# Four units of 448 targets summed from fetched rows as the stationary operand, and routing and experts in one block

## The chip, the cores and the metric

The kernel runs on one core of a Trainium2 chip. The metric is the device time of one execution in microseconds. The engines are TensorE (PE, whose weight loads the profile lists apart as PEld), VectorE (DVE), ScalarE (ACT), GpSimd (POOL) and SyncE (SP), which here only issues DMAs. Each runs its own instructions in order and waits on semaphores.

## What is computed

A layer of a graph transformer on 6,250 nodes with 256 features. Two graph convolutions (`arma_conv`, three steps and two stacks each), an attention block without softmax, and a mixture of six experts of which each node takes two. The part that the change rewrites is the sum over edges in the first convolution:

```python
def arma_conv(x, edge_src, edge_dst, init_w, w, root_w, b, num_layers=T):
    dinv = jnp.where(deg > 0, deg ** (-0.5), 0.0)
    norm = dinv[edge_src] * dinv[edge_dst]
    root = jnp.einsum('nf,kfg->nkg', x, root_w)
    for t in range(num_layers):
        h = (jnp.einsum('nf,kfg->nkg', x, init_w) if t == 0
             else jnp.einsum('nkf,kfg->nkg', out, w))
        msg = h[edge_src] * norm[:, None, None]
        h = jax.ops.segment_sum(msg, edge_dst, num_segments=n)
        out = jax.nn.relu(h + root + b[None])
    return out.mean(axis=1)
...
xn = _layernorm(x)
x = x + gnn(xn, edges) + mix(xn)
x = x + moe(_layernorm(x))      # softmax router, top 2 of 6 experts, three layers each
```

There are 106,250 edges (50,000 random ones in both directions and a loop at each node), sorted by target.

## The kernel before

Nodes lie in 49 tiles of 128 (`TILES`), or in 14 windows of 448 (`WIN`), two of which make a pair of 7 tiles. A table of features holds, for each node, 2 x 128 features in fp16 as a high and a low part, 512 values in all. The stages follow one another:

- *Preparation* (to about 334 us): the layer norm, the root products, the attention sums, and on the side the lists of edges.
- *Build* (334 to 1030 us): PE builds the dense 6272 x 6272 adjacency matrix in fp16 from one-hots (196-column matmuls, L1821 and L1825, a fresh 128x128 load before each), stores it window by window as `adj_d`, and sums the convolution's first step from it (L1836).
- *Pass 0 and pass 1* (`quick_pass`, 1035.8 to 1552.3 and to 2078.5 us): the second and third step of the first convolution. Here the targets are parted. Targets of the dense windows (5 to 13, 9 in all, `DENSE`) are summed by `tile_sums`: for each of 49 source tiles, four matmuls (two stacks, two parts) with the features as 128x128 stationary operand and 448 columns of `adj_d` moving (L1886). The first 2,304 targets, 18 tiles (`SPARSE`), are summed without the matrix: GpSimd fetches the rows of 128 edges' sources by an indirect DMA into one of 16 buffers `got` (L1345), DVE makes a 128x128 one-hot of the edges' targets (L1632), and PE multiplies: one-hot stationary, the 512 fetched values moving (L1932). Two tiles (a duo) share 36 such chunks, 324 a pass; four chunks of a duo serve both tiles, so there are 360 matmuls. Window 5 overlaps these targets by 64 columns, so its matmuls have 384 columns.
- *Late passes* (2078.5 to about 2858 us): the second convolution, all 14 windows dense, in hardware loops, with PE running freely.
- *Decode and routing* (`final`), then *experts* in a block of their own: each token's row is scattered twice into its experts' regions (`row_d`) and 38 slots of 384 rows are computed.

The code of passes 0 and 1 is unrolled. `Course` sets its order: for each step x (a window's tile; 9 x 49 = 441 steps a pass) it says which chunk, transpose and row product follow the tile's four matmuls. Chunks start after step 28. After a tile's last chunk, ACT and DVE scale its sums (`sums_high`, `sums_low`), PE transposes them (`sums_turned`, L1940), DVE adds the root (`sums_hidden`), and PE makes the next features (`row_products`, L1899, in pass 1 L1901 and L1904) in one of two PSUM banks, which ACT and DVE read out (L1427, L1639). A dense window ends with six DVE operations (`finish`).

SP refills `stage0` in pieces of 7 tiles (784 KB, L1314), counted through both passes, 63 a pass. For piece M it waits until PE has used M - 6 pieces (`p_free`). Between them it loads roots and stores pass 0's new features (`some_out`, L1299) to `later_d`. GpSimd begins pass 1 only when all those stores have landed (`t_rows`). A flag makes the kernel take `slow_pass` where a tile has more edges than its chunks hold.

## Time and profile before

| what | us |
|---|---|
| median of 3 runs (3478.55 to 3478.9) | 3478.65 |
| the profiled execution | 3479.78 |
| its span, first to last instruction | 3477.8 |
| build, 333.7 to 1029.7 | 696.0, PE busy 675.85 |
| pass 0, 1035.8 to 1552.3 | 516.5, PE busy 459.98 |
| pass 1, 1552.3 to 2078.5 | 526.2, PE busy 478.63 |
| late passes, 2078.5 to 2858.0 | 779.5, PE busy 773.39 |
| decode and routing, 2858.0 to 3140.8 | 282.8, PE busy 178.09 |
| experts, 3140.8 to the end | 337.0, PE busy 322.51 |

PE is busy for 91% of the span. Its matmuls overlap, so one that is listed with 0.35 us may follow its neighbour after 0.19 us: the starts tell the pace, not the durations. "Idle before" is the time for which an engine had nothing to run ahead of an instruction, with what ended it; "issue" means that nothing that the profile shows was waited for.

### The profile page before, as it was taken

Reading aid. Unit: us, or ns where it says so; the run is one execution under the profiler, and the core shown is the slowest. Engines: PE = TensorE matmul, PEld = TensorE weight load, DVE = VectorE, ACT = ScalarE, POOL = GpSimd, SP = SyncE. Lnnn points to the kernel's source line nnn. Section 1 sums busy time; section 2 is a strip of 40 time slices with the busy share of each in tenths; the row PEclk is TensorE's granted clock in tenths of the full one; section 3 lists DMA queues with packets and bytes.
Section 4 is the critical chain, followed back from the end, with each engine's and each line's share of the span. In section 5 each row is a group of like instructions: output and inputs, shape, how many; then the busy total and the mean of one; then the engine's idle time right before and its main releaser. Section 6 shows DMA issues by size and latency. Waiting matters only on the chain. (4 is left out here: it accounts for less than half of the span.)

```text
span 3477.8 us, 48392 instructions
## 1 busy us (share of the span) xinstructions
PE 3163.9 (91%) x16879; PEld 1851.0 (53%) x16880; DVE 1374.4 (40%) x5337; ACT 787.6 (23%) x1656; POOL 923.7 (27%) x912
## 2 busy tenths in 40 slices
PE   7798999999998898898999999999999999728998
PEld 3464666566554444454455555555555556516775
DVE  7846777777732222221222221222221005433443
ACT  3444555555520000000000000000000003313332
POOL 2000000000006666636666630000000000454555
PEclk9897999999998999999999999999999999869999
DMA  7212465556457666756666668888889995336886
GB/s 185 72 65 85 149 235 208 179 198 234 179 234 246 196 222 203 235 179 203 211 211 223 212 188 291 291 290 292 291 292 319 303 302 160 118 111 168 204 203 138
DMA packets 252700, 723.78 MB, mean 208 GB/s; under 512 B 36437, under 2 KB 159817, under 8 KB 250472
## 3 DMA queue, kind: packets, MB, share of 16 engines
q1 hardware_dynamic: 184298, 595.84, 51.1%
q0 software_dynamic: 53216, 112.76, 11.7%
q10 hardware_dynamic: 15006, 12.82, 1.3%
q8 instruction: 109, 1.79, 0.2%
q14 instruction: 71, 0.58, 0.0%
HBM read 543.01 MB, written 189.34 MB: 211 GB/s over the span
## 5 line engine op out<-in xcount | busy, mean ns | idle before, releaser
L1886 PE MATMUL first_sum<-stage,split 128*128 128x448 f16 (+1 forms) x4508 | 933.3, 355 | 31.4 <-issue 29.1
L1886 PEld LDWEIGHTS first_sum<-stage,split 128*128 128x128 f16 x4508 | 443.6, 99 | 448.4 <-issue 63.7
L1886 PE MATMUL first_sum<-stage,other 128*128 128x448 f16 (+1 forms) x3136 | 664.8, 354 | 15.7 <-issue 15.5
L1836 PE MATMUL first_sum<-stage,other 128*128 128x448 f16 x2744 | 649.9, 354 | 0.2 <-ACT stage L1360 0.2
L1345 POOL DMA_INDIRECT stage<-fresh_d,lane_two x324 | 308.4, 952 | 1117.2 <-DMA fresh_d<-split 942.0
L1886 PEld LDWEIGHTS first_sum<-stage,other 128*128 128x128 f16 x3136 | 309.6, 99 | 298.3 <-issue 35.4
L1360 ACT ACTIVATE stage<-group_ps 128x392 f16<-128x392 f32 x784 | 385.4, 497 | 297.9 <-PE group_ps L1825 294.7
L1345 POOL DMA_INDIRECT stage<-later_d,lane_two x324 | 307.7, 950 | 220.4 <-issue 71.5
L1513 DVE TENSOR_SCALAR place<-iota_col,rel 128x196 f16<-128x196 f16 x1568 | 348.8, 265 | 0.0
L1836 PEld LDWEIGHTS first_sum<-stage,other 128*128 128x128 f16 x2744 | 254.0, 98 | 139.5 <-issue 2.0
L1932 PE MATMUL group_ps<-stage,place 128*128 128x512 f16 x720 | 265.8, 385 | 11.3 <-issue 7.3
L1510 DVE TENSOR_TENSOR lanes<-iota_two,lane_two 128x256 f16<-128x256 f16 x784 | 225.0, 287 | 83.3 <-PE group_ps L1825 71.5
L1821 PE MATMUL group_ps<-place,lanes 128*128 128x196 f16 x784 | 199.9, 255 | 33.4 <-DVE place L1513 14.7
L2247 POOL IOTA ids<- 128x49 f32 x1 | 0.2, 173 | 841.2 <-POOLq L1233 841.2
L2751 POOL DMA_INDIRECT out<-slot_out,slot_idx x114 | 176.5, 1548 | 163.9 <-DMA out<-slot_out,slot_idx 92.7
L1632 DVE TENSOR_SCALAR place<-iota_col,lane_two 128x128 f16<-128x128 f16 x720 | 145.8, 272 | 156.8 <-PE group_ps L1932 111.9
L1825 PE MATMUL group_ps<-place,lanes 128*128 128x196 f16 x784 | 200.9, 257 | 0.0
L2360 ACT ACTIVATE dT<-d_ps,rel 128x448 f32<-128x448 f32 x14 | 8.8, 633 | 843.2 <-PE d_ps L2278 814.1
L1710 DVE TENSOR_TENSOR stage<-first_sum,stage 128x448 f32<-128x448 f32 x42 | 26.2, 625 | 390.7 <-PE first_sum L1886 377.0
L1821 PEld LDWEIGHTS group_ps<-place,lanes 128*128 128x128 f16 x784 | 77.7, 99 | 113.5 <-ACT stage L1360 43.5
L2716 DVE TENSOR_TENSOR slot_out<-out_ps,other 128x256 f32<-128x256 f32 x114 | 48.4, 425 | 185.7 <-PE out_ps L2826 180.0
L2263 POOL DMA_INDIRECT row_d<-rows,seat_idx x84 | 83.8, 998 | 126.0 <-DVE seat_idx L2526 101.9
(387 smaller groups left out, 3052.6 us busy)
## 6 DMA issues: line engine op xcount, KB each, us to landing
stage<-adj_d SPq DMA_DIRECT2D x420, 784.0 KB
adj_d<-stage SPq DMA_DIRECT2D x14, 5488.0 KB, 18.5
row_d<-slow_rows SPq DMA_DIRECT2D x12, 3340.5 KB
other<-pack_d SPq DMA_DIRECT2D x38, 898.0 KB
slot_rows<-row_d SPq DMA_DIRECT2D x38, 393.0 KB
stage<-root_d SPq DMA_DIRECT2D x18, 448.0 KB
xnT_d<-other SPq DMA_DIRECT2D x14, 448.0 KB
split<-root_d SPq DMA_DIRECT2D x14, 448.0 KB, 3.8
```

What stands on the lines that cost most here:

```text
L1345: nc.gpsimd.indirect_dma_start(got[:, g % GOT, :, :].rearrange("p s c -> p (s c)"), None, tables_d[t].rearrange("p j s c -> (p j) (s c)"), ...
L1360: nc.scalar.activation(stage[w % 2][:, :, at * G:(at + 1) * G], group_ps[g % BANKS][:, 0:COLS].rearrange("p (d h) -> p h d", d=G), ACT.Cop ...
L1510: nc.vector.tensor_tensor(lanes[:, u % 4, :, :], iota_two[:, :, :], lane_two[:, bass.ds(g, 1), :].broadcast_to([P, P, 2]), ALU.is_equal)
L1513: nc.vector.tensor_scalar(place[:, 2 * u % RING + s, :], iota_col[:, 0:Q4], rel[:, :, :, :].rearrange("p q s g -> p (q s g)")[:, bass.ds(p ...
L1632: nc.vector.tensor_scalar(hot[:, h % HOTS, :], iota_col[:, s % 2 * P:s % 2 * P + P], tab_key[:, at:at + 1], None, ALU.is_equal).then_inc(s ...
L1821: mm(group_ps[u % BANKS][:, 0:Q4], lanes[:, u % 4, :, 0], place[:, 2 * u % RING, :], start=True, stop=True, skip_group_check=True)
L1825: return mm(group_ps[u % BANKS][:, Q4:COLS], lanes[:, u % 4, :, 1], place[:, 2 * u % RING + 1, :], start=True, stop=True, skip_group_check ...
L1836: m = mm(acc[b][k][:, 0:WIN], other[:, h, half, k * P:(k + 1) * P], stage[b][:, h, :], start=(h == 0 and half == 0), stop=(h == TILES - 1 ...
L1886: m = mm(acc[b][k][:, lo:WIN], side(t)[:, h, part, k * P:(k + 1) * P], ring[:, i, r, lo:WIN], start=(h == 0 and part == 0), stop=(h == TIL ...
L1932: m = mm(group_ps[S % 2][:, :], hot[:, h % HOTS, :], got[:, g % GOT, :, :].rearrange("p s c -> p (s c)"), start=(n == SPANS[s % 2][0]), st ...
L2263: nc.gpsimd.indirect_dma_start(row_d[:, :], bass.IndirectOffsetOnAxis(ap=seat_of[:, j, which:which + 1], axis=0), rows[:, j, :], None).the ...
L2751: nc.gpsimd.indirect_dma_start(out[:, :], bass.IndirectOffsetOnAxis(ap=idx[:, b, t:t + 1], axis=0), done[:, b, t, :], None, bounds_check=N ...
```

## The change

*Targets.* The parted targets are now 4 whole windows ("units") of 448, 1,792 in all. The dense windows are 4 to 13, ten, all 448 wide, so a pass has 490 steps and 70 pieces. A unit is 4 strips of 112 targets with 17 chunks each: 16 x 17 = 272 fetches a pass.

*Chunk.* The fetched rows are the stationary operand (four 128x128 blocks: two stacks, two parts) and the one-hot of 112 targets moves: four matmuls of 112 columns. The sums come out with features on the partitions, so the transposes and the scaling on ACT go; DVE finishes a strip in three operations (`strip_finish`). There are 8 buffers for fetched rows instead of 16, and GpSimd also waits for the former fetch into the same buffer.

*Order.* `Course` has TAIL 22 for 14 and LEAD 10 for 7. The table's parts are stored by pair (`pair_out`), after the load of the piece with the same number; a piece number is now `x // PT + PIECES + 1`, where it was `x // PT + PIECES - 1`.

*Routing and experts.* The experts' instructions follow the routing's on each engine in the same block, and all 98 scatters are in one sequence on GpSimd. SP waits for a semaphore that DVE raises when the table of slots is ready. Buffers of the experts lie in `split`'s space, PSUM banks are shared.

```diff
-SPARSE = 18
-FIRST_DENSE = SPARSE * P // WIN
-CHUNK = 36
-SPANS = (range(0, 19), range(15, CHUNK))
+UNITS = 4
+STRIP = 112
+STRIPS = WIN // STRIP
+CHUNK = 17
+LISTED = UNITS * STRIPS * CHUNK
...
-        return x // PT + PIECES - 1
+        return x // PT + PIECES + 1
...
-                def some_out(n):
-                    if n < PARTED:
-                        sp.wait_ge(s_rows, n + 1)
+                def pair_out(pair):
+                    if pair < UNITS // 2:
+                        sp.wait_ge(s_rows, pair + 1)
                     else:
-                        sp.wait_ge(d_rows, n - PARTED + 1)
-                    js = slice(SOME[n][0], SOME[n][-1] + 1)
+                        sp.wait_ge(d_rows, pair - UNITS // 2 + 1)
+                    js = slice(pair * SUB, (pair + 1) * SUB)
                     sp.dma_start(tables_d[1][:, js, :, :], other[:, js, :, :]).then_inc(t_rows, 16)
...
-                        for some in range(len(SOME)):
-                            if M == stored_at(some):
-                                some_out(some)
                         if M >= PIECES:
                             sp.wait_ge(p_free, M - (PIECES - 1))
                             sp.dma_start(ring[:, i, :, :].rearrange("p t n -> p (t n)"), adj_d[DENSE[n], :, i * PT * WIN:(i + 1) * PT * WIN]).then_inc(p_in[i], 16)
...
+                        for pair in range(PAIRS):
+                            if M == stored_at(pair):
+                                pair_out(pair)
...
-                        if g >= GOT:
-                            pool.wait_ge(s_used, g - (GOT - 1))
-                        at = listed_at(c)
+                        if g >= RING:
+                            pool.wait_ge(s_used, g - (RING - 1))
+                            pool.wait_ge(s_row[g % RING], 16 * (g // RING))
...
+                def strip_finish(t, s):
+                    S, at = t * PARTED + s, s % STRIPS * STRIP
+                    one = hid_s[:, :, s % (2 * STRIPS) * STRIP:(s % (2 * STRIPS) + 1) * STRIP]
+                    ps = group_ps[S % 2][:, :].rearrange("p (k c) -> p k c", k=2)[:, :, 0:STRIP]
+                    if s % STRIPS == 0:
+                        dve.wait_ge(s_in, 32 * (t * UNITS + s // STRIPS + 1))
+                    dve.wait_ge(s_used, t * LISTED + (s + 1) * CHUNK)
+                    nc.vector.tensor_tensor(one, ps, dinv_s[:, at:at + STRIP].unsqueeze(1).broadcast_to([P, 2, STRIP]), ALU.mult).then_inc(s_ev, 1)
+                    dve.wait_ge(s_ev, S + 1)
+                    nc.vector.tensor_tensor(one, one, rin_s[:, :, at:at + STRIP], ALU.add).then_inc(s_v, 1)
+                    dve.wait_ge(s_v, S + 1)
                     nc.vector.tensor_scalar(one, one, 0.0, None, ALU.max).then_inc(s_hid, 1)
...
                 def chunk(t, c):
                     g = t * LISTED + c
-                    pe.wait_ge(s_row[g % GOT], 16 * (g // GOT + 1))
-                    for s in tiles_of(c):
-                        S, n, p = t * SPARSE + s, c % CHUNK, PRODUCTS.index((c, s))
-                        h = t * len(PRODUCTS) + p
-                        if n == SPANS[s % 2][0] and S >= 2:
-                            pe.wait_ge(s_v, S - 1)
-                        pe.wait_ge(s_hot, h + 1)
-                        m = mm(group_ps[S % 2][:, :], hot[:, h % HOTS, :], got[:, g % GOT, :, :].rearrange("p s c -> p (s c)"),
-                               start=(n == SPANS[s % 2][0]), stop=(n == SPANS[s % 2][-1]), skip_group_check=True)
+                    s, first = divmod(c, CHUNK)
+                    S = t * PARTED + s
+                    if first == 0 and S >= 2:
+                        pe.wait_ge(s_ev, S - 1)
+                    pe.wait_ge(s_hot, g + 1)
+                    pe.wait_ge(s_row[g % RING], 16 * (g // RING + 1))
+                    for k in range(2):
+                        for part in range(2):
+                            m = mm(group_ps[S % 2][:, k * D:k * D + STRIP], got[:, g % RING, part, k * P:(k + 1) * P], hot[:, g % HOTS, :],
+                                   start=(first == 0 and k == 0 and part == 0), stop=(first == CHUNK - 1 and part == 1), skip_group_check=True)
                     m.then_inc(s_used, 1)
...
-                    for n in range(BATCHES - 1):
+                    for n in range(BATCHES):
                         scattered(n)
+                    slots.gpsimd(pool)
...
+                    dve.sem_inc(l_table, 1)
+                    slots.vector(dve)
```

PE at the start of pass 0's chunks, before; L1932 is a chunk, L1886 the dense sums of one tile (x4):

```order
L1932 MATMUL group_ps<-stage,place 128x512
L1886 MATMUL first_sum<-stage,split 128x384 x4
L1932 MATMUL group_ps<-stage,place 128x512
L1886 MATMUL first_sum<-stage,split 128x384 x4
L1932 MATMUL group_ps<-stage,place 128x512
```

The same place after; L1874 is a chunk, L1832 the dense sums:

```order
L1874 MATMUL group_ps<-place,stage 128x112 x4
L1832 MATMUL first_sum<-stage,split 128x448 x4
L1874 MATMUL group_ps<-place,stage 128x112 x4
L1832 MATMUL first_sum<-stage,split 128x448 x8
L1874 MATMUL group_ps<-place,stage 128x112 x4
```

One matmul became four, the first window's tiles are wider, and chunks lie further apart (1.62 steps for 1.23).

SP around the end of pass 0, before; `later_d` is the table of pass 1, and its last store is the second of these:

```order
L1299 DMA later_d<-other 128x2048
L1314 DMA stage<-adj_d 128x3136 x3
L1299 DMA later_d<-other 128x3584
L1314 DMA stage<-adj_d 128x3136
L1280 DMA stage<-root_d 128x2x448
```

The same after; the last row here is the last store:

```order
L1267 DMA later_d<-other 128x3584
L1275 DMA stage<-adj_d 128x3136 x3
L1247 DMA stage<-root_d 128x2x448
L1248 DMA stage<-dinv_d 128x448
L1275 DMA stage<-adj_d 128x3136 x2
L1267 DMA later_d<-other 128x3584
```

The last store stood ahead of piece 71, the ninth of a pass of 63, and now stands behind piece 80, the eleventh of a pass of 70.

GpSimd from the last routing to the experts, before; `row_d` takes the tokens' rows, `out` the experts' results:

```order
L2263 DMA row_d<-rows,seat_idx 39168x262 x84
L2211 UNCONDITIONAL_BRANCH
L2739 UNCONDITIONAL_BRANCH
L2743 DMA row_d<-rows,seat_idx 39168x262 x14
L2751 DMA out<-slot_out,slot_idx 6250x256 x114
```

The same after:

```order
L2195 DMA row_d<-rows,seat_idx 39168x262 x98
L2676 DMA out<-split 6250x256 x114
```

The last 14 scatters stood behind the block's end and now follow the others.

## Rows read from the trace of the kernel before

**Rows 1.** Busy us (x count) of PE, PEld, DVE, ACT, POOL, by stage; clock, DMA.

```profile
333.70:1029.70 696.00, 675.85 (x4376) 413.36 (x4376) 498.22 (x2305) 373.92 (x772) 0.00 (x0) 0.99 0.57 204
1035.80:1552.30 516.50, 459.98 (x2339) 238.16 (x2340) 131.52 (x506) 29.42 (x63) 308.40 (x324) 0.96 0.64 214
1552.30:2078.50 526.20, 478.63 (x2542) 262.69 (x2540) 130.91 (x518) 38.11 (x112) 307.72 (x324) 0.96 0.65 207
```

**Rows 2.** PE's dense matmuls in a late pass; then the timeline (start, us) in pass 0.

```profile
2700.00:2840.00 140.00, 140.00 (x742) 1.00 0.92 303
...
1197.29 0.38 PE L1932 MATMUL group_ps<-stage,place 128*128 128x512 f16 x1
...
1198.26 0.38 PE L1932 MATMUL group_ps<-stage,place 128*128 128x512 f16 x1
1198.47 0.38 PE L1940 MATMUL group_ps<-ident,stage 128*128 128x128 f32 x2
1198.69 0.92 PE L1886 MATMUL first_sum<-stage,split 128*128 128x448 f16 x4
```

**Rows 3.** Timeline of PE in pass 1's first window, four 384-column matmuls left out.

```profile
1586.01 0.38 PE L1932 MATMUL group_ps<-stage,place 128*128 128x512 f16 x1
...
1586.87 0.38 PE L1932 MATMUL group_ps<-stage,place 128*128 128x512 f16 x1
```

**Rows 4.** Timeline of PE in the build, two 448-column matmuls left out.

```profile
403.10 0.25 PE L1825 MATMUL group_ps<-place,lanes 128*128 128x196 f16 x1
...
403.56 0.25 PE L1821 MATMUL group_ps<-place,lanes 128*128 128x196 f16 x1
```

**Rows 5.** Timeline of PE in the ranking, one 6-column matmul (L2331) left out.

```profile
2945.48 0.18 PE L2332 MATMUL rank_ps<-chosen,g_ones 128*128 128x42 f16 x1
...
2945.53 0.18 PE L2332 MATMUL rank_ps<-chosen,g_ones 128*128 128x36 f16 x1
```

**Rows 6.** PE's waits (us, times, longest): four of pass 0, then three of pass 1.

```profile
PE first_sum L1886 <- issue: 19.9, 44, 1.0
PE pj L1899 <- DVE other L1639: 10.0, 5, 3.2
PE pj L1899 <- issue: 5.9, 4, 2.5
PE group_ps L1940 <- DVE stage L1612: 5.7, 2, 3.6
...
PE first_sum L1886 <- issue: 15.5, 20, 1.7
PE pj L1901 <- issue: 11.9, 8, 3.6
...
PE group_ps L1940 <- DVE stage L1612: 2.6, 2, 2.3
```

**Rows 7.** Timeline of PE 20 us after pass 1's first fetch.

```profile
1590.12 0.32 PE L1886 MATMUL first_sum<-stage,other 128*128 128x384 f16 x1 [1.03 <-issue]
```

**Rows 8.** Timeline at the start of pass 1: store, first two fetches, first chunk.

```profile
1565.34 0.33 SPq L1299 DMA_DIRECT2D later_d<-other  x1
...
1570.25 0.94 POOL L1345 DMA_INDIRECT stage<-later_d,lane_two  x1 [46.84 <-DMA later_d<-other]
1571.50 0.94 POOL L1345 DMA_INDIRECT stage<-later_d,lane_two  x1 [0.31 <-issue]
...
1577.37 0.61 PE L1932 MATMUL group_ps<-stage,place 128*128 128x512 f16 x1 [4.05 <-DMA stage<-later_d,lane_two]
```

**Rows 9.** Timeline at the end of routing: seats, scatters, rows, transposes.

```profile
3109.51 0.17 DVE L2526 CAST seat_idx<-seat 128x14 uint32<-128x14 f32 x1
...
3117.04 0.96 POOL L2743 DMA_INDIRECT row_d<-rows,seat_idx  x1 [13.08 <-POOLq L2211]
...
3136.39 6.56 SPq L2663 DMA_DIRECT2D slot_rows<-row_d  x4
...
3140.86 1.54 PE L2801 MATMUL t_ps<-ident,slot_rows 128*128 128x128 f32 x6 [42.90 <-DVE slot_rows L2694]
```

More of the change, by code:

```diff
@@ L1 @@
+from collections import namedtuple
 from contextlib import ExitStack
@@ L2351, in _ @@
                     ranked(BATCHES - 1)
+                    slots.tensor(pe)
                 @block.scalar
@@ new lines, in slot_engines @@
+    spot = Carve(slot_space)
+    rows = spot.take(BUF, ST, RW)
+    meta = spot.take(BUF, ST, 4)
+    share = spot.take(BUF, 3, ST)
+    done = spot.take(BUF, ST, D)
+    idx = spot.take(BUF, ST, dt=mybir.dt.uint32)
+    space = Carve(spare)
+    pack = space.take(BUF, PACK)
+    xlT = space.take(BUF, 2, SLOT)
+    h1 = space.take(2, SLOT)
+    h2 = space.take(2, SLOT)
+    t_ps = [banks[n][:, :].rearrange("p (t k n) -> p t k n", t=2, k=2) for n in range(2)]
+    one_ps = [banks[2 + n][:, 0:SLOT] for n in range(2)]
@@ new lines, in gpsimd @@
+    def gpsimd(pool):
+        for s in range(STEPS):
+            b = s % BUF
+            pool.wait_ge(k_idx, s + 1)
+            if s >= 1:
+                pool.wait_ge(k_sent[(s - 1) % BUF], sent(s - 1))
+            for t in range(ST):
+                pool.wait_ge(k_done, s * ST + (BUF * ST + t + 1))
+                nc.gpsimd.indirect_dma_start(out[:, :], bass.IndirectOffsetOnAxis(ap=idx[:, b, t:t + 1], axis=0), done[:, b, t, :], None,
+                                             bounds_check=N - 1, oob_is_err=False, compute_op=ALU.add).then_inc(k_sent[b], 16)
```

881 lines of the change are left out of this document (391 added, 490 removed).

## The prediction

> **What bounds the kernel now.** I read the stage table first [rows 1]: each figure is a busy time inside a stretch, and the reader should see that in the two passes that the change rewrites, PE is busy 460.0 of 516.5 us and 478.6 of 526.2 us, at a mean granted clock of 0.96, while VectorE is busy for a quarter of it, ScalarE for 6 to 7% and GpSimd for about 60%. PE is the bound, with about 10% of stops in it. So an edit there counts by what it does to PE's stream of matmuls, then by what it does to the stops. The third place is the end of routing, where PE stands still for 43 us and a queue on GpSimd sets the time [rows 9].
>
> **Prices of the stream.** A matmul of 448 columns comes every 140/742 = 0.1887 us where nothing stops it [rows 2]. In pass 0 chunk follows chunk at 0.97 us with four such matmuls between, so one chunk (one 512-column matmul) costs 0.97 - 0.755 = 0.215 us. Two fp32 transposes take 0.22 us. With 384 columns the period is 0.86 us [rows 3], so such a matmul costs (0.86 - 0.215)/4 = 0.161 us.
>
> **Dense part, added.** The dense windows go from 9 to 10 and the first is no longer narrowed. Per pass: 196 more matmuls x 0.1887 = 37.0 us, and 196 that grow from 384 to 448 columns, 196 x 0.0277 = 5.4 us. Together +42.4 us, all on PE, nothing hides it.
>
> **Sparse part, replaced.** Gone are 360 x 0.215 = 77.4 us a pass. In their place come 272 chunks of four matmuls with 112 moving columns and a new 128x128 fp16 weight load each. No row shows this shape. From above: a 196-column matmul with its own load costs 0.46 - 2 x 0.1887 = 0.083 us [rows 4]; the row left out there is the two. From below: in the ranking of the router two such pairs of load and matmul, with 6 and 36 or 42 columns, take 0.05 us, 0.025 us each [rows 5], so the load as such needs no more than that. On the line through the 196- and the 448-column rows (0.419 ns a column) 112 columns cost 0.083 - 84 x 0.000419 = 0.048 us. I take that, since the load's 0.025 us fits beneath it. A chunk is 0.191 us and 272 are 52.0 us: -25.4 us a pass. The bounds are 27.2 us (all at 0.025) and 90.3 us (all at 0.083).
>
> The Trainium skill, "TensorE: Matmul & The Clock Gate", section "Back-to-back issue gap", speaks against this edit: it gives a sustained spacing of about 81 ns for pairs of weight load and 128-column matmul. By that figure a chunk would be about 0.32 us, an estimate, and both passes together 72 us dearer than I sum. The trace's 25 ns pairs disagree for small columns, and no row tests a long run of them.
>
> **Transposes, removed.** 36 a pass, 18 pairs x 0.22 = 4.0 us. The waits before them, 5.7 us in pass 0 and 2.6 us in pass 1 [rows 6], go as well: a strip's sums already have features on the partitions, so DVE alone stands between the last chunk and the row product, eight tiles (6 us) later. DVE's mean operation in pass 0 is 131.5/506 = 0.26 us [rows 1], so its three are about 1 us, covered. What is late next is the row product's wait for the previous row (10.0 us in pass 0, [rows 6]); it is not touched, and I leave it. ScalarE only loses work. DVE's one-hots fall from 360 to 272 a pass and are looked ahead by 10 tiles rather than 7; DVE is 25% busy, so nothing.
>
> Stream: 42.4 - 25.4 - 4.0 = **+13.0 us a pass**.
>
> **Stops inside the passes.** [rows 6] has 25.8 us of "issue" in pass 0 (19.9 + 5.9) and 27.4 us in pass 1 (15.5 + 11.9): PE stands before a matmul that waits for nothing shown. [rows 7] is one, in the middle of a tile, where no semaphore stands. The build stage issues 4,376 matmuls and as many loads in 696 us, 12.6 instructions a us, against 9.1 in pass 0 (2,339 and 2,340) and about 12.2 in the new one (6,096 for sums and chunks and 360 for row products in some 528 us), and it is busy 97% without gathers [rows 1]. So rate alone does not stop PE; gathers have a part. If the stops go with gathers (324 to 272) they shrink by 16%; if with PE's instructions in the pass (4,248 to 6,096) they grow by 44%. That is -4 to +11 us in pass 0 and -4 to +12 us in pass 1. I take +4 in each, between the two.
>
> **Supply of rows.** GpSimd issues a gather every 1.25 us [rows 8], 405 us for 324; the new 272 need 340 us. PE wants one every 440/272 = 1.62 tiles, at least 1.62 x 0.755 + 0.191 = 1.41 us, so supply is faster than demand (before, 0.97 to 1.2 us against 1.25, evened out by 16 buffers). But there are only 8 buffers now, and GpSimd has a second wait before each. A row set must land within 8 x 1.41 = 11.3 us of its buffer's release; the first gather of pass 1 takes 7.1 us from issue to use [rows 8]. I charge nothing, with 4 us to spare.
>
> **Start of pass 1.** GpSimd's gathers wait until the table of pass 1 is stored. Now SP issues the last store after 15 tiles, at 1565.34; the first gather starts 4.9 us later, PE's first chunk 7.1 us after that, and PE has waited 4.05 us [rows 8]. In the new order SP issues that store behind the load of piece 80, whose wait lets go when PE has done 4 pieces, 28 tiles, of pass 1. PE is at its first chunk one tile later. So PE waits 4.9 + 7.1 = 12 us and, with a 784 KB load ahead of the store on the queue, up to 3.5 us more, against 4.0: +8 to +11.5 us. I take **+9.5 us**. SP's other moved steps (the roots of a unit, behind a wait for its last strip) come 14 tiles after that strip and 13 before the next finishes; no cost.
>
> **End of routing.** The block boundary sent the last 14 scatters behind the last DVE operation: seats are known at 3109.68, the first scatter starts at 3117.04 [rows 9]. They wait for the seats alone now, and start at about 3110.0, as GpSimd has been idle for 13.08 us when it starts them. The chain behind, 19.35 us from the first of them to the load of rows and 4.5 us to PE, moves with it: **-7.0 us**. The weights' loads follow the table, some 13 us ahead of the rows. What precedes the passes changes by one gather and some small copies beside a busy PE: within 1 us.
>
> **Sum.** Pass 0: 13.0 - 5.7 + 4 = +11.3. Pass 1: 13.0 - 2.6 + 9.5 + 4 = +23.9. End: -7.0. Together +28.2 on the profiled run's 3479.8 us is 3508.0; that run is 1.1 us above the median, so **3507 us**.
>
> **Rivals.**
> 1. *The gathers' stops shrink, and it ends faster.* Half as many gathers are in flight. If the stops come from a deep queue of them (those at the pass starts, such as [rows 7], come some 20 us after 16 gathers went out), half of 25.8 + 27.4 us goes, and half of the clock's loss, (1 - 0.96) x 1042.7 = 41.7 us. That is -27 - 21 - 8 (my +4s) = -56: 3451. With a quarter instead of a half it is 3475. It ends faster than before from some 36 us on. Against it: stops of 0.7 us are spread over all of the pass. Chance 0.13.
> 2. *Eight buffers are too few.* If landing takes over 11.3 us, PE waits at each turn of the ring: 34 turns a pass, at 1 us each +68 us, 3575; half of that gives 3541. For it: DMA share 0.64, with loads of 784 KB in the way. Against it: 7.1 us. Chance 0.13.
> 3. *Weight loads are not covered* in a run of four: at the bound of [rows 4], 2,176 x (0.083 - 0.048) = +76 us, 3583. Chance 0.07. This is the skill's rule above, priced from a row.
> 4. *It does not do what it says*: a strip with over 17 x 128 = 2,176 edges would send everything down the long path. 106,250/6,250 = 17 edges a target make 1,904 of 112 targets plus up to 15; chance below 0.01.
>
> **Chances.** My sum 0.60, within 3490 to 3530 (its terms' bounds: stops -8 to +23 against +8, store 8 to 11.5). Rivals as above, 0.07 for what I don't see. The range 3474 to 3565 leaves out most of rival 1 and 3 and the top of 2. A measurement of this kernel tells about 0.2%, 7 us, from no change. Faster by more: 0.11. Within: 0.10. Slower: 0.79.
>
> **What would show it.** Right: chunks spaced in the new passes so that four 112-column matmuls take about 0.19 us; passes of about 528 and 550 us; one wait of 12 to 16 us before the first chunk of pass 1; no gap between the seats and the last scatters. Wrong: 0.3 us a chunk (rival 3), waits of PE on the fetched rows all through (2), or "issue" stops well under 26 us a pass and a clock near 1.0 (1).

## The result: faster by 3.3%, where slower was forecast

The changed kernel takes 3362.7 us (median of 4 runs, 3358.3 to 3368.7), the kernel before 3478.6 us beside it (4 runs, 3476.5 to 3478.9). The ratio is 0.967, 95% interval 0.966 to 0.969: 116 us less. The forecast was 3507 us, 28 us more.

One fact is needed to understand everything below, and I learned it only from the experiments: the same kernel takes two kinds of time on different chips. The kernel before took 3478.6 us here, 3456.6 and 3462.0 us on a second chip and 3453.9 us on a third; on two others it took 3276.4 us, both times. (The record does not number the first chip; I take it for one of its own by its time.) The profile that the prediction was made from is of the first kind. I call the first kind a *chip with stops* and the second a *chip without*, since PE's unexplained stops are what differs most. A kernel is compared only with kernels on the same chip, or with the same kernel's stages on the other kind.

Busy time by stage after the change, columns as in [rows 1] (start:end, length, PE, PEld, DVE, ACT, POOL, clock, DMA share, GB/s); the three lines answer to those three:

```profile
331.00:1022.00 691.00, 674.03 (x4388) 411.77 (x4388) 500.74 (x2323) 377.05 (x779) 0.00 (x0) 0.99 0.58 206
1028.70:1480.80 452.10, 448.90 (x3228) 268.39 (x3229) 115.63 (x417) 21.13 (x45) 262.21 (x272) 1.00 0.73 247
1480.80:1965.30 484.50, 471.87 (x3427) 291.16 (x3425) 113.89 (x429) 29.98 (x94) 262.01 (x272) 0.99 0.69 223
```

Pass 0 is 64.4 us shorter (516.5 to 452.1), pass 1 41.7 us (526.2 to 484.5), although PE issues 38% more matmuls in pass 0. PE is busy 99% of pass 0 where it was 89%, at a granted clock of 1.00 where it was 0.96. All that is left of PE's waits (us in total, times, longest) in pass 0, and then in pass 1; compare [rows 6]:

```profile
PE first_sum L1832 <- DMA split<-fresh_d: 2.2, 1, 2.2
PE first_sum L1832 <- issue: 1.9, 3, 1.0
PE pj L1846 <- issue: 0.9, 1, 0.9
PE pj L1846 <- DVE other L1588: 0.3, 1, 0.3
...
PE group_ps L1874 <- DMA stage<-later_d,lane_two: 9.8, 1, 9.8
PE group_ps L1874 <- issue: 1.8, 2, 1.4
PE first_sum L1832 <- issue: 0.8, 2, 0.5
```

Before the change there was more "issue" than the prediction counted. Its 25.8 us for pass 0 came from [rows 6], whose first row there leaves out the first 28 us or so of the pass (the 2.3 us stops among them), and both passes have lines that it does not show. Over the whole passes, pass 0 first:

```profile
PE first_sum L1886 <- issue: 29.1, 51, 2.3
PE group_ps L1932 <- issue: 1.2, 3, 0.5
PE group_ps L1940 <- issue: 1.1, 2, 0.6
...
PE group_ps L1932 <- issue: 6.1, 10, 1.4
PE pj L1904 <- issue: 3.3, 5, 1.0
```

With the 5.9 us of L1899, and the 15.5 and 11.9 us of pass 1, that is 37.3 and 36.8 us before, and 2.8 and 2.6 us now. The rest of the program hardly moved: from the first late pass to the first matmul of decoding 814.6 and now 815.7 us, from there to the end 585.1 and 576.7; the passes begin 7.1 us earlier. (The late passes' matmuls run some 32 us beyond the end that the tables ahead of the prediction give them.)

The stream itself does what was forecast. PE's timeline in pass 0, answering to [rows 2]:

```profile
1200.51 0.36 PE L1874 MATMUL group_ps<-place,stage 128*128 128x112 f16 x4
1200.70 1.68 PE L1832 MATMUL first_sum<-stage,split 128*128 128x448 f16 x8
1202.22 0.36 PE L1874 MATMUL group_ps<-place,stage 128*128 128x112 f16 x4
1202.41 1.68 PE L1832 MATMUL first_sum<-stage,split 128*128 128x448 f16 x8
```

The dense matmuls start 0.19 us after the first matmul of the chunk ahead of them, and chunks lie 1.71 us apart, the other 1.52 being eight dense matmuls.

Start of pass 1 (last store, first fetch, first chunk), answering to [rows 8], and end of routing (seats, first scatter of the last batch, rows, transposes), answering to [rows 9]:

```profile
1504.37 0.43 SPq L1267 DMA_DIRECT2D later_d<-other  x1
...
1511.69 0.95 POOL L1309 DMA_INDIRECT stage<-later_d,lane_two  x1 [57.49 <-DMA later_d<-other]
...
1514.56 0.53 PE L1874 MATMUL group_ps<-place,stage 128*128 128x112 f16 x4 [9.84 <-DMA stage<-later_d,lane_two]
...
2994.98 0.17 DVE L2461 CAST seat_idx<-seat 128x14 uint32<-128x14 f32 x1
2995.43 0.97 POOL L2195 DMA_INDIRECT row_d<-rows,seat_idx  x1 [5.72 <-DVE seat_idx L2461]
...
3015.12 6.61 SPq L2593 DMA_DIRECT2D split<-row_d  x4
...
3019.65 1.54 PE L2724 MATMUL bank<-ident,split 128*128 128x128 f32 x6 [40.90 <-DVE split L2623]
```

### The profile page after: what moved, and what is told of

Read it like the earlier page. It is cut to its first block and busy times, and to the rows that moved or that the text cites. A ratio compares the mean times of both kernels' runs of the same rounds, so it can differ in the third digit from the quotient of the medians.

```text
span 3357.7 us, 51929 instructions
## 1 busy us (share of the span) xinstructions
PE 3142.1 (94%) x18657; PEld 1906.0 (57%) x18658; DVE 1342.9 (40%) x5159; ACT 771.4 (23%) x1620; POOL 834.9 (25%) x808
## 5 line engine op out<-in xcount | busy, mean ns | idle before, releaser
L1832 PE MATMUL first_sum<-stage,split 128*128 128x448 f16 x4704 | 948.8, 353 | 4.1 <-DMA split<-fresh_d 2.2
L1832 PE MATMUL first_sum<-stage,other 128*128 128x448 f16 x3332 | 688.1, 353 | 0.9 <-issue 0.8
L1832 PEld LDWEIGHTS first_sum<-stage,split 128*128 128x128 f16 x4704 | 449.8, 98 | 376.1 <-issue 6.4
L1782 PE MATMUL first_sum<-stage,other 128*128 128x448 f16 x2744 | 646.7, 353 | 0.2 <-ACT stage L1324 0.2
L1309 POOL DMA_INDIRECT stage<-fresh_d,lane_two x272 | 262.2, 964 | 1094.0 <-DMA fresh_d<-split 934.5
L1832 PEld LDWEIGHTS first_sum<-stage,other 128*128 128x128 f16 x3332 | 315.2, 98 | 246.8 <-issue 4.0
L1309 POOL DMA_INDIRECT stage<-later_d,lane_two x272 | 262.0, 963 | 219.8 <-PE group_ps L1874 102.0
L1874 PEld LDWEIGHTS group_ps<-place,stage 128*128 128x128 f16 x2176 | 160.2, 98 | 111.5 <-issue 12.9
L2676 POOL DMA_INDIRECT out<-split x114 | 177.6, 1558 | 164.0 <-DMA out<-split 90.1
L1874 PE MATMUL group_ps<-place,stage 128*128 128x112 f16 x2176 | 196.8, 213 | 11.7 <-DMA stage<-later_d,lane_two 9.8
L2294 ACT ACTIVATE dT<-bank,rel 128x448 f32<-128x448 f32 x14 | 8.7, 633 | 842.6 <-PE bank L2211 813.7
L1581 DVE TENSOR_SCALAR place<-iota_col,lane_two 128x112 f16<-128x112 f16 x544 | 111.6, 264 | 149.8 <-PE group_ps L1874 131.7
L2195 POOL DMA_INDIRECT row_d<-rows,seat_idx x98 | 98.3, 1003 | 132.3 <-DVE seat_idx L2461 104.2
## 6 DMA issues: line engine op xcount, KB each, us to landing
stage<-root_d SPq DMA_DIRECT2D x28, 448.0 KB
xnT_d<-other SPq DMA_DIRECT2D x14, 448.0 KB
split<-root_d SPq DMA_DIRECT2D x14, 448.0 KB, 3.9
```

The lines of the kernel that those rows point to most:

```text
L1309: nc.gpsimd.indirect_dma_start(got[:, g % RING, :, :].rearrange("p s c -> p (s c)"), None, tables_d[t].rearrange("p j s c -> (p j) (s c)") ...
L1581: nc.vector.tensor_scalar(hot[:, g % HOTS, :], iota_col[:, 0:STRIP], tab_key[:, c:c + 1], None, ALU.is_equal).then_inc(s_hot, 1)
L1782: m = mm(acc[b][k][:, 0:WIN], other[:, h, half, k * P:(k + 1) * P], stage[b][:, h, :], start=(h == 0 and half == 0), stop=(h == TILES - 1 ...
L1832: m = mm(acc[b][k][:, 0:WIN], side(t)[:, h, part, k * P:(k + 1) * P], ring[:, i, r, :], start=(h == 0 and part == 0), stop=(h == TILES - 1 ...
L1874: m = mm(group_ps[S % 2][:, k * D:k * D + STRIP], got[:, g % RING, part, k * P:(k + 1) * P], hot[:, g % HOTS, :], start=(first == 0 and k ...
L2195: nc.gpsimd.indirect_dma_start(row_d[:, :], bass.IndirectOffsetOnAxis(ap=seat_of[:, j, which:which + 1], axis=0), rows[:, j, :], None).the ...
```

## Eight buffers, the second wait, and a chip without stops

My first theory was rival 1 (fewer fetches in flight). Two kernels changed the depth in the kernel before, one gave it the second wait, and the fourth took GpSimd's second wait out of the changed one. All four ran on a chip where the kernel before took 3276.4 us (19 runs).

**b_got8**, eight row buffers in the kernel before, and nothing else:

```diff
-        GOT = 2 * RING
+        GOT = RING
```

> The kernel before with 8 buffers for fetched rows instead of 16, nothing else. Depth theory (the stops of PE in passes 0 and 1 come from how many fetches GpSimd has outstanding): the stops mostly go, pass 0 falls from 516.5 to about 445 us, pass 1 from 526 to about 465 us, the whole to about 3350 us. Rate theory (the old form asks for a row set every 1.14 us where GpSimd gives one in 1.25 us, and the new form every 1.41 us): fewer buffers even out less, so the passes stay or grow, 3480 to 3520 us. Wait theory (it is the second wait before each fetch in the new kernel that paces GpSimd): no change, about 3479 us.

3282.0 us, ratio 1.002 (1.001 to 1.003): 5.6 us slower.

**b_fly4**, 16 buffers but a fetch waits until the one four ahead of it has landed:

```diff
+                        if g >= 4:
+                            pool.wait_ge(s_row[(g - 4) % GOT], 16 * ((g - 4) // GOT + 1))
```

> The kernel before with its 16 buffers, and before fetch g GpSimd waits until fetch g-4 has landed, so at most 4 are in flight. If transfers in flight make the stops: most of the stops go, 3350 to 3400 us. If it is the number of buffers filled ahead and not the flight, or the rate: about 3479 us. If landing takes over 5 us at times, the cap itself costs: up to 3520 us.

3386.6 us (2 runs), ratio 1.033 (1.031 to 1.035). PE now waited for rows (49.3 us in 52 waits in pass 0), so this run tells what too few fetches in flight cost and nothing of the stops.

**b_wait2**, the kernel before with a second wait that is always met:

```diff
+                            pool.wait_ge(s_row[g % GOT], 16 * (g // GOT))
```

> The kernel before with 16 buffers and the new kernel's second wait before each fetch (the former fetch into the same buffer has landed, which is already so). Depth and rate theories: about 3479 us, within 10. Wait theory: 3350 to 3400 us.

3275.7 us, ratio 0.999 (0.998 to 1.000): the wait costs nothing here.

**a_nowait2**, the changed kernel without that wait:

```diff
-                            pool.wait_ge(s_row[g % RING], 16 * (g // RING))
```

> The changed kernel without the second wait before each fetch; the wait for the buffer's last use stays. Depth and rate theories: about 3363 us, within 10. Wait theory: the stops come back, 3440 us or more.

3303.5 us (2 runs), ratio 1.008 (1.006 to 1.010): **slower than the kernel before, by 27.1 us**, where the forecast for the change was 28.2. The stages show why. Both passes of b_wait2, which stands for the kernel before here:

```profile
1024.20:1455.80 431.60, 431.60 (x2340) 236.09 (x2341) 132.91 (x506) 29.59 (x63) 309.14 (x324) 1.00 0.77 257
1455.80:1914.90 459.10, 454.89 (x2538) 258.32 (x2537) 131.32 (x517) 38.65 (x112) 308.45 (x324) 0.99 0.75 237
```

and of a_nowait2, the changed stream:

```profile
1017.60:1465.20 447.60, 447.60 (x3228) 268.22 (x3229) 115.56 (x417) 21.30 (x45) 261.43 (x272) 1.00 0.75 249
1465.20:1946.40 481.20, 471.26 (x3425) 291.18 (x3424) 113.60 (x429) 30.00 (x94) 261.21 (x272) 0.99 0.70 225
```

The same instructions of PE that took 516.5 us in [rows 1] take 431.6 us here, and PE is busy throughout pass 0. So the kernel before lost 85 us in pass 0 (56.5 us idle, 28.4 us of longer busy time) and 67 us in pass 1 to something that this chip does not have; the changed one lost 4.5 and 3.3 us to it. None of these four ran on a chip with stops, so none of them tests what makes the stops.

## What the stops look like

Timeline of PE and GpSimd in the kernel before on the first chip, 20 us into pass 0 (weight loads left out):

```profile
1054.80 0.48 PE L1886 MATMUL first_sum<-stage,split 128*128 128x384 f16 x1 [2.34 <-issue]
1054.83 0.95 POOL L1345 DMA_INDIRECT stage<-fresh_d,lane_two  x1 [0.30 <-issue]
1055.53 0.48 PE L1886 MATMUL first_sum<-stage,split 128*128 128x384 f16 x1 [0.25 <-issue]
1056.08 0.95 POOL L1345 DMA_INDIRECT stage<-fresh_d,lane_two  x1 [0.30 <-issue]
1056.93 0.48 PE L1886 MATMUL first_sum<-stage,split 128*128 128x384 f16 x1 [0.92 <-issue]
...
1057.33 0.95 POOL L1345 DMA_INDIRECT stage<-fresh_d,lane_two  x1 [0.30 <-issue]
...
1058.58 0.99 POOL L1345 DMA_INDIRECT stage<-fresh_d,lane_two  x1 [0.30 <-issue]
1059.75 0.48 PE L1886 MATMUL first_sum<-stage,split 128*128 128x384 f16 x1 [2.35 <-issue]
1061.85 0.48 PE L1886 MATMUL first_sum<-stage,split 128*128 128x384 f16 x1 [1.62 <-issue]
...
1215.77 0.94 POOL L1345 DMA_INDIRECT stage<-fresh_d,lane_two  x1 [2.31 <-DMA split<-runs_d,start]
```

GpSimd puts out one fetch after another, every 1.25 us. PE gets one matmul at a time, 0.7 to 2.8 us apart, in the middle of a run of dense matmuls that wait for no semaphore. It recovers soon after GpSimd's run of 16 ends. GpSimd stops as well: the last row is one such stop. The profile puts it down to a DMA that had landed before the passes; the chunk that frees this fetch's buffer was done 8 us earlier. Some of PE's waits are for VectorE, and these too are missing in b_wait2, so a part of the loss stood under other names in [rows 6].

## The same pair elsewhere; one part alone; fetches or packets

These four ran on a chip with stops (kernel before 3456.6 us, 19 runs). **a_same** is the changed kernel.

> The changed kernel itself, beside the kernel before. Two pictures of the chip are known: on one the kernel before took 3478.6 us, with about 65 us of PE's idle time that no wait explains (the stops), on another 3276.4 us, with none. Theory S (the change's gain is the end of the stops, its stream costs what was forecast): on a chip without stops this kernel is SLOWER than the one before, by 20 to 30 us (3297 to 3307 beside 3276), pass 0 longer by 12 to 18 us; on a chip with stops it is faster by 110 to 120 us (3360 beside 3478). Theory C (the change is faster by itself, whatever the chip): the ratio is 0.96 to 0.975 everywhere.

3350.0 us, ratio 0.970 (0.968 to 0.971): 106.6 us less. Theory S holds in the main: the sign depends on the chip. (On a chip without stops the changed kernel ran only as a_nowait2 and, below, a_early, each with a small edit.) Pass 0 takes 448.0 us, as on the chip without stops.

**b_one** is the kernel before with the changed kernel's routing and experts in one block (its `final` and `slot_engines`).

> The kernel before with only the last part of the change: routing and experts one block, everything ahead of them as before. The prediction charged it -7.0 us: 3269 beside 3276 on a chip without stops, 3472 beside 3479 on one with stops. If the stops hung on anything in how the program is laid out (its length, its blocks), the part of the kernel ahead of the routing, which is instruction for instruction that of the kernel before, would change too: passes 0 and 1 then differ by more than 5 us from those of before on the same chip.

3450.4 us, ratio 0.998 (0.997 to 0.999): -6.2 us (2 to 11 by the interval) for -7.0 forecast. Passes 0 and 1 keep their stops (512.4 and 519.6 us).

**a_early**, the changed kernel with its stores two pieces earlier and ahead of the ring's load:

```diff
-                    at = courses[0].piece_after(courses[0].row_at[(pair, SUB - 1)])
+                    at = courses[0].piece_after(courses[0].row_at[(pair, SUB - 1)] + 2) - 2
```

> The changed kernel with the stores of the second table's pair rows put back where the kernel before has them in SyncE's order (ahead of the ring load, two pieces earlier). The prediction charged the later place 9.5 us at the start of pass 1. Theory: PE's wait there (9.8 us after the change) falls to 2 to 4 us and the kernel is 5 to 8 us faster than the changed one on the same chip. Rival: the store then waits for rows that come later anyway, the ring's loads wait behind it, and nothing is won (within 2 us).

3337.3 us against 3350.0, ratio to before 0.966 (0.964 to 0.968): 12.7 us less, more than either theory had. In the profiles 9.4 us of it are in pass 1; the passes also begin 3.8 us earlier, which the edit does not explain. The store goes out at 1488.54 and the first fetch at 1493.47; of PE's wait of 9.9 us for rows 1.1 are left, and 3.3 us more stand as "issue" before the first chunk.

**b_lane96**, fetches of 96 rows in the kernel before, with the other 32 rows of each buffer zeroed once ahead of the passes (I wrote of 360 fetches a pass; it issues 324 for 360 matmuls, so 31,104 packets a pass, where the changed kernel has 34,816):

```diff
-                        nc.gpsimd.indirect_dma_start(got[:, g % GOT, :, :].rearrange("p s c -> p (s c)"), None, tables_d[t].rearrange("p j s c -> (p j) (s c)"),
-                                                     bass.IndirectOffsetOnAxis(ap=tab_row[:, at:at + 1], axis=0)).then_inc(s_row[g % GOT], 16)
+                        nc.gpsimd.indirect_dma_start(got[0:96, g % GOT, :, :].rearrange("p s c -> p (s c)"), None, tables_d[t].rearrange("p j s c -> (p j) (s c)"),
+                                                     bass.IndirectOffsetOnAxis(ap=tab_row[0:96, at:at + 1], axis=0)).then_inc(s_row[g % GOT], 16)
```

> The kernel before with each of its 360 fetches a pass cut from 128 to 96 rows (34560 packets a pass, where the changed kernel has 34816 and the kernel before 46080); the missing rows are zero, so part of the sums is left out. The count of instructions of every engine stays. Theory G (the stops come from the load of the row fetches): on a chip with stops PE's unexplained idle time in passes 0 and 1 falls from about 65 us to under 20 and the kernel is 60 us or more faster (under 3420 beside 3478). Theory I (they come from the count of PE's and GpSimd's instructions or from what they do): it stays within 15 us of the kernel before. On a chip without stops both give 3270 to 3280 beside 3276, and the run tells them not apart.

3457.9 us, ratio 1.000 (0.999 to 1.002). With fewer packets than the changed kernel all stops are there (pass 0 511.3 us). Theory G falls.

## The count of fetches decides

Same chip, kernel before 3462.0 us (7 runs).

**b_got8x** repeats b_got8. (It too has eight buffers only; the second wait that the text speaks of is not in it.)

> The kernel before with the changed kernel's 8 row buffers and its second wait, once more, now beside b_skip4. On the chip without stops (before: 3276 us) it cost 5.6 us. Theory D (the stops of PE come with fetches that run up to 16 ahead): on a chip with stops (before: 3450 to 3480 us) it is at least 40 us faster than the kernel before. Rival (depth has nothing to do with them): it stays within 10 us of it, or loses 5. On a chip without stops: 3282 beside 3276 again.

3437.9 us, ratio 0.993 (0.991 to 0.995): 24 us less, where the two passes of the kernel before lose some 140 us on this chip. Depth has a part, a small one; neither theory had it right.

**b_skip4**, every fourth fetch left out of the kernel before, its chunk takes the rows of the one ahead:

```diff
+def fetch_of(g):
+    return 3 * (g // 4) + min(g % 4, 2)
...
+                        if g % 4 == 3:
+                            continue
```

> The kernel before with every fourth of its 324 fetches a pass left out; the chunk takes the rows of the one ahead of it, so part of the sums is wrong rows' sums. GpSimd issues 243 fetches a pass (the changed kernel 272), PE's instructions stay one for one. b_lane96 had 25% fewer packets and the same count of fetches, and the stops stayed. Theory N (the stops come with the count of fetches that GpSimd works out, not with what they move): on a chip with stops the kernel is at least 40 us faster. Rival I (they come with PE's own instructions): within 10 us of before. Without stops: 3270 to 3278 beside 3276.

3337.1 us, ratio 0.964 (0.962 to 0.967): **125 us faster, with PE's instructions one for one those of the kernel before.**

**a_more**, 55 more fetches a pass in the changed kernel:

```diff
+                        if c % 5 == 0:
...
+                            nc.gpsimd.indirect_dma_start(more, None, tables_d[t].rearrange("p j s c -> (p j) (s c)"),
+                                                         bass.IndirectOffsetOnAxis(ap=tab_row[:, c:c + 1], axis=0)).then_inc(s_more, 16)
```

> The changed kernel with one more fetch after every fifth, into a buffer that nobody reads: 327 fetches a pass where the kernel before has 324. PE, DVE and ACT have the same instructions as in the changed kernel. Theory N: on a chip with stops they come back, and it is 40 us or more slower than the changed kernel there (3390 or more where that takes 3350 to 3363). Rival I: within 10 us of it. Where there are no stops: within 10 us of the changed kernel's 3297 to 3307.

3478.8 us, ratio 1.006 (1.004 to 1.008): **some 130 us slower than the changed kernel, with its PE instructions.** Pass 0:

```profile
1025.20:1544.20 519.00, 468.71 (x3228) 268.67 (x3229) 117.39 (x419) 21.23 (x45) 315.76 (x327) 0.99 0.70 229
```

and PE's waits in it, the stops back in the changed kernel's own lines:

```profile
PE first_sum L1842 <- issue: 21.2, 47, 1.0
PE group_ps L1884 <- issue: 15.0, 30, 1.0
PE pj L1856 <- issue: 7.7, 12, 1.7
PE pj L1856 <- DVE other L1598: 4.9, 1, 4.9
```

Against the 447.6 us of a_nowait2, all busy, the pass lost 71 us: 50 us idle, 49 of which these rows name, and 21 us of longer busy time, which no wait names.

**a_nowaitx** repeats a_nowait2.

> The changed kernel without GpSimd's second wait, once more, on whatever chip this is. On the chip without stops it took 3303.5 beside 3276.4. Theory W (the second wait holds GpSimd's fetches back and so keeps the stops away): on a chip with stops this kernel is 40 us or more slower than the changed one (3390 or more beside a kernel before of 3457). Rival (the wait does nothing): ratio to the kernel before 0.965 to 0.972 where there are stops, 1.006 to 1.010 where there are none.

3346.2 us, ratio 0.967 (0.965 to 0.970), where the changed kernel had 0.970. The second wait has no part in it.

## Rate, runs, descriptors or GpSimd's time

Another chip with stops (kernel before 3453.9 us, 7 runs).

**b_skip12** leaves out every twelfth fetch: 297 a pass.

> The kernel before with every twelfth fetch left out (297 a pass; that chunk takes the rows of the one ahead, so part of the sums is of wrong rows). With 324 a pass a chip with stops takes about 3460 us, with 243 (b_skip4) 3337. GpSimd puts out fetches back to back every 1.25 us, so 297 are 371 us of work in a pass that needs 431 us, 324 are 405 us. Theory R (PE starves while GpSimd issues without a pause, the harm grows with its share of the time): the time lies between, 3380 to 3430. Rival (a sharp threshold between 272 and 324, at GpSimd's own limit): under 3360 or over 3450.

3387.9 us, ratio 0.982 (0.980 to 0.984). Between the two, as theory R has it; but a fixed limit on how fast GpSimd gives fetches would put it between as well (see the table below).

**b_burst8** is b_skip4 with fetches in groups of eight:

```diff
-                        if f >= GOT:
-                            pool.wait_ge(s_used, last_use(f - GOT) + 1)
+                        if f >= GOT and f % 8 == 0:
+                            pool.wait_ge(s_used, last_use(f + 7 - GOT) + 1)
```

> b_skip4 (243 fetches a pass, 16 buffers) with GpSimd's fetches put out in groups of eight: it waits until eight buffers are free, then issues eight back to back (10 us) and pauses some 4 us. Same count, same packets, same PE instructions as b_skip4 (3337 us beside 3462 before). Theory R' (it is the unbroken run of fetches that starves PE, not their count): the stops come back in part, 30 us or more above b_skip4. Rival (the mean rate decides): within 10 us of b_skip4, 3330 to 3350.

3328.7 us, ratio 0.965 (0.962 to 0.968), no worse than b_skip4. Eight fetches back to back, then a pause, do no harm. GpSimd's timeline:

```profile
1205.78 0.94 POOL L1357 DMA_INDIRECT stage<-fresh_d,lane_two  x1 [0.30 <-issue]
1207.03 0.95 POOL L1357 DMA_INDIRECT stage<-fresh_d,lane_two  x1 [0.30 <-issue]
1212.55 0.99 POOL L1357 DMA_INDIRECT stage<-fresh_d,lane_two  x1 [4.58 <-PE group_ps L1944]
1213.85 0.95 POOL L1357 DMA_INDIRECT stage<-fresh_d,lane_two  x1 [0.30 <-issue]
```

The 12 us that pass 0 of b_skip4 and b_burst8 keeps over the 431.6 us (443.6 and 444.0) lie almost all in one place, 1044 to 1055, near the end of the opening run of 16 fetches; the changed kernel, whose opening run is 8, has no stop there.

**a_more16** is a_more with 16 rows in each extra fetch.

> a_more (the changed kernel with 55 more fetches a pass: 3479 beside 3462 before, and beside 3350 for the changed one), but each extra fetch has 16 rows, an eighth of the packets. Theory P (what harms is GpSimd's time on a fetch, which for 96 rows was 0.93 us and for 128 rows 0.95 us): most of the 130 us stays, over 3420. Rival (descriptors or packets of the extra fetches harm): under 3370.

3477.4 us, ratio 1.007 (1.005 to 1.009): as a_more. Such a fetch holds GpSimd for 867 to 890 ns, one of 128 rows for 960 to 966.

**a_fill** has 110 fills in place of the 55 fetches:

```diff
+                                nc.gpsimd.memset(more, 0).then_inc(s_more, 1)
```

> The changed kernel with, in place of a_more's 55 extra fetches a pass, 110 fills of 128x512 float32 on GpSimd at the same places: about the same extra time on GpSimd, no DMA. Theory B (any work that keeps GpSimd busy brings the stops, through the engine or its port): over 3420. Theory F (only the making of fetches does): within 10 us of the changed kernel, 3340 to 3370 beside 3462, or some us more where a fill makes a fetch late.

3354.6 us, ratio 0.971 (0.970 to 0.973); the changed kernel had 0.970 on its chip. Theory F holds. Pass 0, where GpSimd is busier than in a_more:

```profile
1026.90:1480.50 453.60, 450.76 (x3228) 268.15 (x3229) 122.48 (x417) 21.09 (x45) 320.15 (x382) 0.99 0.73 246
```

So what brings the stops back is neither bytes, nor packets, nor GpSimd's busy time, but fetch instructions.

## Fewer fetches in the scheme of before

On the second chip without stops (kernel before 3276.4 us, 7 runs).

**b_sp14** keeps the scheme of before and sums 14 tiles from fetched rows, 252 fetches a pass:

```diff
-SPARSE = 18
+SPARSE = 14
```

> The kernel before, its scheme kept, with 14 tiles (four windows) in place of 18 summed from fetched rows: 252 fetches a pass, the change's four units without its new form of chunk and without the merged block. By the terms of the prediction its stream is longer than before's by 42.4 us a pass for the dense matmuls and shorter by 17.2 (80 of 360 chunk matmuls at 0.215) and 0.9 (transposes): +24 us a pass. Theory N (the count of fetches decides): pass 0 takes 450 to 460 us on either kind of chip; where there are stops that is 3375 to 3390 beside 3457, faster by 2%; where there are none 3320 to 3330 beside 3276, slower by 1.5%. Rival (the gain needs the new chunk form, fetched rows stationary): 3440 or more where there are stops.

3324.5 us, ratio 1.015 (1.013 to 1.016), pass 0 456.7 us. The price of the wider dense part is confirmed (+25.1 us in pass 0, 24 worked out). It ran on no chip with stops, so that fewer fetches alone would have gained in a kernel with the right sums is likely by b_skip4, not shown.

**a_early_b** repeats a_early.

> The changed kernel with the earlier stores again, beside b_sp14. Where there are stops: ratio to the kernel before 0.963 to 0.968 once more. Where there are none: 3288 to 3296 beside 3276, still slower than the kernel before.

3303.3 us, ratio 1.008 (1.006 to 1.010), 7 to 15 us above what I expected. Its pass 1 is 8.5 us shorter than that of a_nowait2 (472.7 against 481.2), but its passes began 5.9 us later (1023.5 against 1017.6), on another chip; where passes begin varies from 1016 to 1036 among all these profiles without a link to the kernel. On a chip without stops the kernel before stays the best; on one with stops a_early is (0.966), level with the cut-down b_skip4.

Pass 0, us. "Needed every" is the pass without stops divided by the fetches; "came every" is the measured spacing from GpSimd's first fetch of the pass to its last:

| PE's stream | fetches, buffers | needed every | came every, with stops | without | pass 0 with stops | without |
|---|---|---|---|---|---|---|
| before (also b_one, b_lane96; b_wait2) | 324, 16 | 1.33 | 1.46 to 1.49 | 1.26 | 511.3 to 516.5 | 431.6 |
| before (b_got8x, b_got8) | 324, 8 | 1.35 | 1.48 | 1.28 | 499.7 | 437.1 |
| before (b_skip12) | 297, 16 | 1.45 | 1.48 | not run | 472.1 | not run |
| before (b_skip4, b_burst8) | 243, 16 | 1.78 | 1.66, 1.71 | not run | 443.6, 444.0 | not run |
| changed (a_more, a_more16) | 327, 8 | 1.37 | 1.50 | not run | 519.0, 518.8 | not run |
| changed (profile after, a_same; a_nowait2) | 272, 8 | 1.65 | 1.55, 1.54 | 1.53 | 452.1, 448.0 | 447.6 |

The middle columns show something that I had overlooked. Back to back, a fetch starts every 1.25 us on either kind of chip, and without stops GpSimd keeps this up through the whole pass. On the chips with stops no pass came below 1.46 us, because GpSimd itself stops: in the profile before it starts 48 fetches late in pass 0, most of them eight or nine fetches apart, 64 us in all (late: over 0.6 us behind both the fetch ahead and the chunk that frees the buffer); in b_wait2 it starts none late. It goes on doing so in the changed kernel (65 late fetches, 66 us, against 2 in a_nowait2), where PE hardly loses time. So on these chips the loss appears just where PE's stream wants a fetch more often than about every 1.48 us (PE's chunks lie 1.24 us apart in b_wait2 and 1.50 us in a_nowait2). That is a relation in the figures, not a mechanism: in the kernel before PE's rows had been asked for 14 us or more ahead of their use, and PE waits for none of them inside the pass.

## Why the prediction was wrong, step by step

- **Stops inside the passes: this step failed.** I took +4 us in each pass, within -4 to +12. They fell by 80 us in pass 0 (85 to 4.5) and by 64 us in pass 1 (67 to 3.3). Two errors lie in it. The first is size: I counted 25.8 us of "issue" where the pass has 37.3 and lost 85, although my own reading of [rows 1] had PE idle for a tenth of the pass (56.5 us). The rest stood as PE's waits for VectorE and as busy time (PE was busy 460.0 us, at a clock of 0.96, for a stream that takes 431.6 at 1.00). It could have been found without a run: 1,568 x 0.1887 + 196 x 0.161 + 360 x 0.215 + 4.0 = 409 us by the prediction's own prices, some 20 for the row products, against 516.5. I priced what the edits change and never the whole stage. The second is the law: I scaled by the count of fetches (-16%) or of PE's instructions (+44%). What the runs show instead is the rate: taking a quarter of the fetches away from the same stream of PE removes the stops (b_skip4), adding 55 to the changed one brings them back (a_more), and they appear where fetches are wanted faster than the 1.46 to 1.50 us that GpSimd manages on such a chip. The prediction worked out the time between demands (0.97 to 1.2 us before, 1.41 after), but for supply alone, and did not connect it with the stops. Why PE stops then stays open.
- **Rival 1** was the right side, at a chance of 0.13: 3451 worked out, 3363 measured. It had the clock right as well ("near 1.0"). Its mechanism, the number of fetches in flight, has a small part (24 us by b_got8x); the number per time has the large one.
- **Stream, +13.0 us a pass: right, 3 us small.** Without stops pass 0 grows by 16.0 us (431.6 to 447.6). A chunk takes the forecast 0.19 us, so 0.048 us a matmul. That disposes of rival 3. The Trainium skill ("TensorE: Matmul & The Clock Gate", section "Back-to-back issue gap") gives some 81 ns for a load and a 128-column matmul. The trace does not agree: in runs of four of 112 columns between dense ones the spacing is 48 ns, and the line through two rows was the better guide.
- **Supply of rows, 0: right.** PE waits for no fetched rows inside the changed passes; rival 2 is out. In the kernel before, eight buffers cost 5.6 us (b_got8).
- **Start of pass 1, +9.5 us: right in mechanism, too large.** Forecast a wait of 12 to 15.5 us, measured 9.84, so +5.8 over the 4.05 of before. The store's way to the first fetch is 7.3 us, within the 4.9 plus up to 3.5 allowed, but the first rows are used 2.9 us after their fetch, not 7.1, though PE stood waiting for them in both. In the old order SP puts out five other loads between the store and that use, in the new one none; a_early, which puts the loads back there, has 7.8 us again. Pass 1 without stops grows by 22.1 us (459.1 to 481.2), near 13.0 + 9.5 = 22.5, but by two misses that cancel: 16 for the stream and 6 for the start. a_early takes 9.4 us out of it, more than PE's wait grew by.
- **Waits ahead of the transposes, -5.7 and -2.6 us.** They were stops under VectorE's name; b_wait2 has none.
- **End of routing, -7.0 us: right.** Seats to PE took 31.35 us [rows 9], now 24.67: -6.7; b_one measured -6.2 by itself.
- **The sum** was right for the other kind of chip: +28.2 forecast, +27.1 measured with a_nowait2. That is luck in part. The prediction was for a profile full of stops; its +8 for them and its -8.3 for the waits ahead of the transposes, neither of which exists on that chip, cancel. The profiles of b_wait2 and a_nowait2 differ by +16.0 and +22.1 in the passes, -8.2 behind them and -6.6 ahead of them, where nothing was forecast.
- The passes begin 7.1 us earlier on the first chip. I forecast nothing there and found no cause; it is within the spread named above.

## What to carry to other kernels

Before you price an edit, price the whole stage by its own undisturbed rows; what is left over is the true size of the stops, whatever names the waits bear. Take the rows over the whole stage, and all of them. If an engine that issues indirect fetches is asked for them nearly as fast as it gives them, treat its rate as a resource of the whole core, measure it over the whole stage rather than between two neighbours, and count fetch instructions, not bytes. And a gain that lives on such a disturbance may have another sign on another chip: run both kernels on more than one.

## What I had not expected of the hardware

- The kernel before takes 3276 us on two chips and 3454 to 3479 on the others. In the traces the difference lies in the passes (152 us over both on the first chip) and in the routing and experts (tail of 585 us in the profile before, 547 in b_wait2), while the late passes, dense matmuls with no fetch beside them, take the same (814.6 and 815.5 us to the first matmul of decoding). The clock explains at most a part: 0.96 for 1.00 over 516.5 us is some 21 us of the 85, an estimate, and a_more loses 71 us at 0.99.
- Where the stops are, they fall at nearly the same matmuls in different runs and chips: counted in PE's records from the start of pass 0, idle time of over 0.3 us gathers near 524, 630, 685, 795, 1060, 1115, 1371 and 1613 in both the profile before and b_one, and in a_more many such places are about 52 records apart. GpSimd's own late fetches are regular too (above). That would fit a late supply of instructions to PE and the other engines alike, held up by the fetches of GpSimd. It is a guess, argued and not shown: I have no run that moves PE's instructions and nothing else.
- On the chips with stops a fetch costs PE time by its being issued, whether it has 16, 96 or 128 rows. Why some chips feel it and others don't stays open. Only one chip was used on two occasions, and it was of the same kind both times, so that it is the chip and not the occasion rests on little.
